# Scores before the second output tile, transposes of the next rows around the stores, and two output products before the logits

## What is computed

```python
# layer 0, h = relu(layernorm(x))
q, k, v = heads(h @ Wq + bq), heads(h @ Wk + bk), heads(h @ Wv + bv)
probs = softmax(q @ k.T / sqrt(128) + where(adj, 0, -9e15))
x = x + (probs @ v) @ Wf + bf
# layer 1, h = relu(layernorm(x))
g = einsum('bnd,ade->bane', h, W); th = tanh(g)
attn = leaky_relu(th @ w_src + (th @ w_dst).T, 0.2)
attn = softmax(where(adj, attn, -999))
f = elu(attn @ g + b)
gate = sigmoid(h @ H_w.T + H_b)
x = x + gate * f + (1 - gate) * h
```

## Time and profile before

| what | value |
|---|---|
| median of 3 runs | 2491.99 us (2491.9 to 2494.87) |
| profiled execution, its own time | 2491.45 us |
| its span | 2489.6 us |
| granted clock of PE, mean | 0.994 |
| busy share PE, PEld, DVE, ACT, POOL | 97%, 69%, 87%, 44%, 34% |
| share of 16 DMA engines, queue q1 | 69.9% |
| chain that ended last | DVE 38%, issue 24%, ACT 10%, SPq 9%, POOL 9%, DMA 6%, PE 5% |

### The profile page before, as it was taken

The page is one execution under the profiler, slowest core; times in us unless marked ns, Lnnn a source line. Parts: engine busy times, 40 slices in busy tenths (PEclk is TensorE's granted clock), DMA queues, the critical chain, the costliest instruction groups (busy, mean ns, idle before and its releaser), DMA issues.

```text
span 2489.6 us, 58759 instructions
## 1 busy us (share of the span) xinstructions
PE 2405.5 (97%) x22408; PEld 1714.1 (69%) x22439; DVE 2176.0 (87%) x3236; ACT 1091.1 (44%) x1416; POOL 852.4 (34%) x589
## 2 busy tenths in 40 slices
PE   7898999999999999999999999999999999999997
PEld 6665676667776667776667776667776667776665
DVE  7867888988988988988988988988988988988968
ACT  6434334444444444444444444444444444444434
POOL 0223233343233343233343233343333343333331
PEclk9999999999999999999999999999999999999999
DMA  7376777776677776677776677776677776677762
GB/s 261 94 179 173 204 190 197 218 212 181 200 192 199 219 212 181 200 189 201 219 212 180 198 190 200 220 211 182 197 190 203 219 211 182 194 193 203 217 157 52
DMA packets 755673, 481.24 MB, mean 193 GB/s; under 512 B 611760, under 2 KB 636336, under 8 KB 755632
## 3 DMA queue, kind: packets, MB, share of 16 engines
q1 hardware_dynamic: 755632, 480.65, 69.9%
HBM read 277.59 MB, written 34.60 MB: 125 GB/s over the span
## 4 chain that ended last, share of the span: by engine, by line
DVE 38%; issue 24%; ACT 10%; SPq 9%; POOL 9%; DMA 6%; PE 5%; DVEq 1%; POOLq 0%; ACTq 0%
POOL arena L2644 4%; SPq L663 4%; DVE arena L1710 3%; SPq L669 3%; DVE arena L1545 3%; PE pair_prj L902 3%; DMA arena<-arena 3%; DVE bn_out L1421 3%; DVE arena L1534 2%; DVE arena L1542 2%; DVE arena L1531 2%; ACT arena L2246 2%; ACT arena L2248 2%; DVE max L1853 2%; POOL rstd L2618 2%
## 5 line engine op out<-in xcount | busy, mean ns | idle before, releaser
L902 PE MATMUL pair_prj<-w_hi,arena 128*128 128x256 f16 (+1 forms) x3432 | 810.7, 326 | 25.3 <-DVE p_place L1599 20.4
L902 PE MATMUL pair_prj<-w_lo,arena 128*128 128x256 f16 (+1 forms) x1716 | 559.6, 326 | 0.0
L902 PEld LDWEIGHTS pair_prj<-w_hi,arena 128*128 128x128 f16 x3432 | 337.0, 98 | 255.3 <-issue 32.7
L928 PE MATMUL pair_prj<-arena,w_hi 128*128 128x256 f16 x2376 | 394.2, 273 | 3.3 <-DVE arena L1465 2.3
L2649 POOL TENSOR_TENSOR arena<-arena 128x768 f32<-128x768 f32 x60 | 108.8, 1813 | 777.3 <-DVE arena L1710 555.3
L928 PE MATMUL pair_att<-arena,w_hi 128*128 128x256 f16 x2160 | 360.0, 273 | 0.0
L928 PE MATMUL pair_prj<-arena,w_lo 128*128 128x256 f16 x1188 | 324.5, 273 | 0.0
L928 PE MATMUL pair_att<-arena,w_lo 128*128 128x256 f16 x1080 | 294.4, 273 | 0.0
L1226 PE MATMUL pair_prj<-w_hi,arena 128*128 128x384 f16 x870 | 255.0, 326 | 2.8 <-DMA w_lo<-forms 1.6
L928 PEld LDWEIGHTS pair_prj<-arena,w_hi 128*128 128x128 f16 x2376 | 228.6, 98 | 30.2 <-DVE arena L1465 2.6
L902 PEld LDWEIGHTS pair_prj<-w_lo,arena 128*128 128x128 f16 x1716 | 168.6, 98 | 108.8 <-issue 1.4
(11 more groups left out here) (275 smaller groups left out, 4985.0 us busy)
## 6 DMA issues: line engine op xcount, KB each, us to landing
w_hi<-forms SPq DMA_DIRECT2D x353, 288.0 KB, 3.9
w_lo<-forms SPq DMA_DIRECT2D x353, 288.0 KB, 4.7
arena<-in_x SPq DMA_DIRECT2D x63, 768.0 KB, 4.8
out<-arena SPq DMA_DIRECT2D x64, 384.0 KB, 2.3
arena<-arena SPq DMA_DIRECT2D x31, 768.0 KB, 3.7
arena<-arena SPq DMA_TRANSPOSE x372, 3.3
forms<-w_lo SPq DMA_DIRECT2D x14, 288.0 KB, 3.2
forms<-w_hi SPq DMA_DIRECT2D x10, 288.0 KB, 3.5
```

Source lines behind the costliest of these rows:

```text
L902: mm = nc.tensor.matmul(pair[:, lo:hi], lhs(a, k), weight(m, k, b)[:, lo:hi], start=(k == 0 and n == 0), stop=(k == KT - 1 and n == 2))
L928: mm = nc.tensor.matmul(pair[:, c * 256:(c + 1) * 256], weight(m, k, a)[:, o:o + P], (ht0_hi, ht0_lo)[b][:, k, :], start=(k == 0 and n == ...
```

## The change

On DVE, in the loop and in step 2, the scores and their shift stand before the ELU and gate of tile 1. In step 2 the gate terms T3 and T2 are taken behind `output_first(1)`, and T1 and T4 behind `p0_low`. On SP, in the loop, the transposes of the next rows stand around the second store, and the load of `x1` between the transposes of the high and of the low probabilities. In step 2 the stores of gate terms and quarters and the loads of forms go behind the transposes. On PE `form_product(i, 1)` stands before `logits`.

```diff
@@ SP @@
+                def load_x1():
+                    after_alone(sp, eye_made, full_made[1], 2 * j + 2)
+                    after_alone(sp, eye_made, x1_moved, DMA * (2 * j + 2))
+                    sp.dma_start(x1, x_g[i]).then_inc(x1_moved, DMA)
+
                 if last:
                     store(p, 0)
+                if mid and seven_gate(j):
+                    after_held(sp, transposes_held, v_psum, 2 * i + 2)
+                    transpose_rows(0, 0, ht0_hi, i + 1)
                 if last:
                     store(p, 1)
+                if mid and seven_gate(j):
+                    transpose_rows(0, 1, ht0_lo, i + 1)
                 if now and mid:
                     after_alone(sp, eye_made, out_stored, 2 * DMA * j)
                     sp.dma_start(keep, x1).then_inc(x1_moved, DMA)
-                    if seven_gate(j):
-                        after_held(sp, transposes_held, v_psum, 2 * i + 2)
-                        transpose_rows(0, 0, ht0_hi, i + 1)
-                        transpose_rows(0, 1, ht0_lo, i + 1)
-                    after_alone(sp, eye_made, full_made[1], 2 * j + 2)
-                    after_alone(sp, eye_made, x1_moved, DMA * (2 * j + 2))
-                    sp.dma_start(x1, x_g[i]).then_inc(x1_moved, DMA)
-                if third:
-                    store_gate_lows((T1, T4))
-                    first_forms()
+                    if not seven_gate(j):
+                        load_x1()
                 if now and not first:
                     after_held(sp, transposes_held, p0_gaps, i)
                     after_held(sp, transposes_held, p0_hi_made, i)
                     transpose_blocks(pt0[0], e0[0], pt0_landed)
+                    if mid and seven_gate(j):
+                        load_x1()
                     after_held(sp, transposes_held, p0_lo_made, i)
                     transpose_blocks(pt0[1], e0[1], pt0_landed)
...
                 elif third:
-                    store_gate_quarters()
-                    gate_residents()
+                    store_gate_lows((T1, T4))
+                    first_forms()
                 if seven(i):
                     late_forms()
+                if third:
+                    store_gate_quarters()
...
                 if mid:
                     first_probabilities(j, j + 1)
+                if third:
+                    gate_residents()
@@ PE @@
                     form_product(i, 0)
+                    form_product(i, 1)
                     logits()
-                    for n in range(1, 4):
+                    for n in range(2, 4):
                         form_product(i, n)
@@ DVE @@
                 if third:
                     gate_terms()
-                    low_gate_term(T3)
-                    low_gate_term(T2)
...
                 if third or (last and mid and seven_gate(j)):
                     output_first(1, p)
+                if third:
+                    low_gate_term(T3)
+                    low_gate_term(T2)
...
                 if nxt and not second:
                     offset(0, i + 1)
+                if early_values:
+                    scaled_scores()
+                    shift0()
                 if last:
                     output_elu(1, p)
                     output_gated(1, p)
-                if now:
-                    if not early_values:
-                        low_values(0)
+                if early_values:
+                    low_values(1)
+                    normal0()
+                    p0_low()
+                elif now:
+                    low_values(0)
                     if second:
                         dve.wait_ge(forms_stored, TERMS_STORED)
                     scaled_scores()
                     shift0()
-                    if third:
-                        low_gate_term(T1)
-                        low_gate_term(T4)
-                    if nxt and not second:
-                        low_values(1)
                     normal0()
-                    if second or not nxt:
-                        low_values(1)
+                    low_values(1)
                     p0_low()
+                if third:
+                    low_gate_term(T1)
+                    low_gate_term(T4)
```

## The result

The changed kernel takes **2541.99 us** in the median of 4 runs (2538.66 to 2550.12), the kernel before beside it 2492.52 (4 runs, 2491.9 to 2494.87): a ratio of 1.0202, 95% interval 1.0176 to 1.0227. It is 49.5 us **slower**. The forecast was 2475 us, and the range of 2455 to 2502 does not hold it.

A forecast was written before the change was run, and what follows sets the result against it. PE, nearly full, was taken to follow DVE. Loop: 31.1 us of waits go, 20.2 come, 10.9 less, rounded to 9.5; with 7 for i=2, 16.5 off 2491.45 gives 2475 us, range 2455 to 2502 (8 in 10).

The forecast's parts named there:

- part 3: SP's queue in the loop: PE's 0.37 us wait for the transposed low probabilities goes; landed about 1218.5, cover 0.9 us.
- Parts 1 and 2: DVE and ACT: scores first remove PE's 0.52 us wait before project_h(1), by 0.2 us; DVE's normalising product precedes POOL's.
- Rival (a): POOL's product beats DVE's normalising product and holds DVE; PE waits at product 1: 34 us more, 2509 us; chance 0.2.
- part 2: ACT no longer late; DVE's normalising product starts 0.1 us before POOL's, so p0_low ends at 1211.9 instead of 1212.88.
- Parts 4 and 5: gate_quarter(6) ends at 1227.36, so PE, with product 1 before the logits, newly waits 0.84 us; 0.12 us hiccup goes.
- Part 4: DVE up to gate_quarter(6): anchored by PE's gate form 2, then without a gap for 8.86 us, ending at 1227.36.
- Part 6: Third stage (i=2), once: waits before low_values(1), for transposed probabilities and late loads shrink; net 7 us, 4 to 9.
- Rival (c): Low probabilities land after 1220.2 as copy, x1 load and transposes crowd, or product 1's wait cancels gains: 2491 us, chance 0.15.

The follow-up runs named there:

- SP's part alone: The changed kernel with DVE's and PE's loop orders put back as before, keeping SP's new loop order and the changed step 2: 2531.25 us.
- 2465.83: The changed kernel with the x1 load behind both transpose pairs, POOL's biases behind target_terms and DVE's sums, logits between products 0 and 1: 2465.83 us.
- all but PE's part: The changed kernel with the logits back between output products 0 and 1, all else as changed: 2522.03 us.
- step 2 alone: The kernel before, with its DVE, SP and PE loop orders kept and only step 2 as changed: 2488.77 us.
- the load later still: The kernel with 2465.83 us, with the x1 load moved another place back, behind the weight quarter that gate form 6 reads: 2500.36 us.

## Why the prediction was wrong

**The step that failed is part 3, "The 0.37 us wait goes, cover 0.9 us".** It has two terms.

- The low pair's issue. Part 3 has the two high transposes "at 1210.3 to 1213" and the low ones "until 1216.4". They start at 1210.1, as said, but take 3.87 us, as the copy to `keep` is issued 0.73 us ahead of them. The low pair ends at 1235.69 - 18.13 = 1217.56, 1.2 us later. Before, the transposes of the next rows stood between the copy and these, and the earlier trace rows show 5.59 us for all four. I took a duration from a row whose neighbour the change removes.
- From issue to PE. Part 3 has 2.1 us, from rows in which the load of `x1` is ahead of all four transposes. Directly ahead of the low pair it makes 3.6 us. This is the other 1.5 us. SP's part alone shows 3.8. The load put behind brings the landing back and removes the wait, with the high pair's issue as slow as here. So the first term used up the cover of 0.9 us, and the load, by its own place between the pairs and by the late landing, made the wait. (That run also moved POOL's bias, which PE's `context(0)` does not wait for.)

The landing was forecast at 1218.5 and came at 1221.17, 2.7 us later: 1.8 us behind where PE was to want it, instead of 0.9 us ahead. Where the forecast took off the loop's 16.7 us, 38.8 us came on top of them. Part 3 also had the load of `x1` land 1.3 us later than before; it landed 2.8 us later (1216.62 before, 1237.58 - 18.13 = 1219.45 now). POOL waits for it, 51 us in all, but PE's `logit_operands` does not.

Point by point:

- **Parts 1 and 2 hold.** The bias takes 0.23 us, two of the four output steps alternate with POOL and take 2.28 us, PE does not wait at `project_h(1)` after i=3, and DVE was in first, by 0.55 us where part 2 had 0.1: `normal0` takes 0.96 us. Rival (a) did not come. But DVE's order alone, without SP's, would have cost 150 us; the forecast never priced that its second store holds SP's queue, since both moved together.
- **Parts 4 and 5: the wait came, its reason was another.** Forecast 0.84 us, because DVE could reach `gate_quarter(6)` no earlier than 1227.36. Measured up to 0.52 in 25 iterations, 11.8 us in all, hung on `context(0)`. Part 4's "from there DVE works without a gap" holds for the earlier trace rows, and yet `context_low` has no room there: it starts at 1222.38, 2.1 us behind `context(0)` of the earlier trace rows, and 2.0 us is what it takes in the changed kernel where it waits for ACT (1239.30 to 1241.32). The price of the order is 13 us where only it is changed, and 20 in the changed kernel. The sum had 20.2; with the wait and its reason both off, that this fits is luck. The row of `context_low` in the kernel before:

```profile
1222.38 1.01 DVE L1667 SCALAR_TENSOR_TENSOR arena<-pair_att,arena 128x384 f16<-128x384 f32 x2
```

- **Part 6** had 7 us, between 4 and 9. It is 4.
- **Rival (c)** is what happened: copy, load and transposes crowded, and the landing moves. It was priced at 2491 us by the assumption that the wait would only come back to what it was. No row bounded the landing from above, and the range should have held that bound.
- **The clock** was in no case. Iterations with a piece at 1.2 GHz make some 11 us or a little more of the 49.5.

The number itself was not far off what the change would do with SP in order: with the load behind the transposes and POOL held, both products still ahead of the logits, it is 2471.67 us against the forecast 2475. Part of that is luck: the loop there gives 18 us where the forecast had 9.5, and step 2 gives 4 where it had 7.

## What to carry to other kernels

When an order of DMAs is changed, price each against its new neighbours: the duration of an issue and the time to land belong to what stands directly ahead of it on the queue, and a row of the old order shows the old neighbour. A large load goes behind the small transfers that the busiest engine waits for, but each place further back has to be tried: one more cost 35 us here. Work on a port that two engines share goes behind a semaphore, not behind the landing of a transfer. Before an engine's work is moved ahead of a wait, follow that wait back: if the chain starts at the engine's own earlier step, arriving earlier wins nothing, and independent work (here the logits) belongs in the gap.

## What the runs showed of the hardware

- **A pair of transposes behind a copy.** 3.87 us to issue when a 768 KB copy is issued 0.73 us ahead, 2.75 when it is 3.8 us ahead. The other pairs of probabilities take 2.6 to 3.0.
- **A landing behind a load.** 3.6 and 3.8 us from the end of the low pair's issue to PE's start with 768 KB from DRAM directly ahead, 2.1 us where four transposes follow the load. From issue to landing it is 5.2 and 5.1 us against 3.4, and 3.3 with the load put behind.
- **A race decided by a landing.** The end of the load of `x1` differs by up to 1.3 us between iterations, and 0.06 us decides whether POOL or DVE is in first. That makes some 74.1 or 75.6 us of an iteration. The eight runs of that kernel lie 10 us apart, the four with POOL on a semaphore 4 us (17 runs of the kernel before lie 8 us apart).
- **The clock and short waits.** The stretches at the low granted clock in the loop are 0 before and in the kernels with 2465.83 and 2471.67 us. They are 9 where PE waits 2.0 and 0.5 us in an iteration, 7 and 5 where it waits 2.0 and 1.8 us for the landing (all but PE's part, SP's part alone), one in the kernel with step 2 alone (i=3, where the landing costs 2.1 us), 3 where it waits some 2 us at product 1 in 17 iterations, and one in each of the 28 where it waits 4.9 us. With a wait of 1.35 us in each iteration (the load later still) the profiled execution has none. So waits of about 2 us can come with a cost beyond their length: in the changed kernel some 11 us beside 35.
